# Graph attention on one core: scores computed with keys on the partitions, mask and sums on GpSimd

## The reference, cut to what matters

```
proj = x @ W                      # W: 256 x 512
Wh, Ws = split(proj, 2)           # 4096 x 256 each
scores = Wh @ Ws.T                # 4096 x 4096
a = softmax(scores, axis=-1) * adj
out = leaky_relu(a @ Wh + x, 0.01)
```

## Time and profile before

| | us |
|---|---|
| median of 3 runs | 2951.92 |
| lowest and highest run | 2949.37 to 2952.56 |
| span of the profiled execution, first to last instruction | 2948.1 |
| TensorE busy | 2849.7 (97%) |
| VectorE busy | 2153.3 (73%) |
| ScalarE busy | 1362.9 (46%) |
| GpSimd busy | 567.3 (19%) |

### The profile page before, as it was taken

How to read it: one execution, slowest core, us unless ns; L and a number is a source line. 1 busy time by engine, 2 the same in 40 slices (tenths; PEclk the granted TensorE clock), 3 DMA queues, 4 the chain that set the end, 5 groups by cost and what they waited for, 6 DMA issues and landing times. The chain is left out here.

```text
span 2948.1 us, 52591 instructions
## 1 busy us (share of the span) xinstructions
PE 2849.7 (97%) x16880; PEld 2497.7 (85%) x16880; DVE 2153.3 (73%) x3960; ACT 1362.9 (46%) x2417; POOL 567.3 (19%) x213
## 2 busy tenths in 40 slices
PE   4799999999999989999999999998999999999999
PEld 2699999999999978788888888887888888888888
DVE  7888888888888855666666666665566666676666
ACT  4566666666666646333333333334333333333333
POOL 5544545545544502000000000001100000000000
PEclk7899999999999999999999999999999999999999
DMA  2222222222222206333333333333533333333332
GB/s 97 82 75 78 80 70 74 82 71 78 75 72 78 75 30 225 102 103 104 107 100 98 97 104 100 107 102 101 161 100 104 102 109 103 112 111 102 103 104 72
DMA packets 120646, 283.62 MB, mean 96 GB/s; under 512 B 12816, under 2 KB 58640, under 8 KB 120592
## 3 DMA queue, kind: packets, MB, share of 16 engines
q1 hardware_dynamic: 113600, 264.29, 29.3%
q0 software_dynamic: 5120, 16.78, 1.7%
q10 hardware_dynamic: 1872, 1.84, 0.2%
HBM read 249.30 MB, written 33.55 MB: 96 GB/s over the span
## 5 line engine op out<-in xcount | busy, mean ns | idle before, releaser
L91 PE MATMUL l0b_acc<-l_h_parts,l0b_turned_hi 128*128 128x512 f32 x1984 | 759.2, 415 | 0.0
L480 POOL TENSOR_SCALAR l_adj_pieces<-l_adj_pieces 128x1024 f32<-128x1024 f32 x124 | 480.8, 3878 | 492.5 <-DMA l_adj_pieces<-in_adj_dram 492.3
L92 PE MATMUL l0b_acc<-l_h_parts,l0b_turned_lo 128*128 128x256 f32 x1984 | 556.5, 280 | 0.0
L498 ACT CAST l0b_turned_hi<-l0b_turn_psum 128x512 fp32r<-128x512 f32 x512 | 299.1, 585 | 340.6 <-PE l0b_turn_psum L663 335.6
L584 DVE TENSOR_TENSOR l0b_turned_lo<-l0b_turn_psum,l0b_turned_hi 128x512 fp32r<-128x512 f32 x512 | 351.7, 687 | 126.1 <-ACT l0b_turned_hi L498 122.4
L91 PEld LDWEIGHTS l0b_acc<-l_h_parts,l0b_turned_hi 128*128 128x128 f32 x1984 | 374.2, 189 | 66.2 <-issue 0.2
L1059 ACT CAST g1b_turned_hi<-g1b_turn_psum 128x512 fp32r<-128x512 f32 x256 | 149.9, 586 | 522.2 <-PE g1b_turn_psum L1173 521.7
L1059 ACT CAST g0b_turned_hi<-g0b_turn_psum 128x512 fp32r<-128x512 f32 x256 | 149.9, 585 | 521.2 <-PE g0b_turn_psum L1173 520.7
L92 PEld LDWEIGHTS l0b_acc<-l_h_parts,l0b_turned_lo 128*128 128x128 f32 x1984 | 375.1, 189 | 0.0
L91 PE MATMUL g1b_acc<-g_wh_parts,g1b_turned_hi 128*128 128x512 f32 x992 | 361.0, 398 | 0.6 <-DVE g1b_turned_lo L1098 0.5
L91 PE MATMUL g0b_acc<-g_wh_parts,g0b_turned_hi 128*128 128x512 f32 x992 | 361.0, 398 | 0.1
(11 more groups left out here) (191 smaller groups left out, 5708.1 us busy)
## 6 DMA issues: line engine op xcount, KB each, us to landing
g_adj_pieces<-in_adj_dram SPq DMA_DIRECT2D x256, 512.0 KB, 3.9
l_adj_pieces<-in_adj_dram SPq DMA_DIRECT2D x128, 512.0 KB, 3.9
g_wh_tile<-wh_tiles SPq DMA_DIRECT2D x64, 256.0 KB, 2.7
wh_tiles<-g0a_stage POOLq DMA_DIRECT2D x32, 256.0 KB, 3.3
wh_tiles<-g1a_stage POOLq DMA_DIRECT2D x32, 256.0 KB, 3.8
l0b_x_in<-in_x_dram SPq DMA_DIRECT2D x32, 128.0 KB, 3.2
x_rows<-l0b_x SPq DMA_DIRECT2D x32, 128.0 KB, 3.1
g0a_rows<-x_rows SPq DMA_DIRECT2D x8, 512.0 KB, 4.1
```

The costliest lines, as they stand in the source:

```text
L91: pe.matmul(out, lhs_hi, rhs, start=first, stop=False)
L92: return pe.matmul(out[:, width:], lhs_lo, rhs[:, :width], start=False, stop=False)
L480: pool.tensor_scalar(adj_pieces[:, q, :], adj_pieces[:, q, :], 0.0, PENALTY, ALU.is_le, ALU.mult).then_inc(penalty_ready, 1)
L498: act.copy(turned_hi[:, s % RING, :], turn_psum[:, s % RING, :]).then_inc(hi_ready, 1)
```

## The change

In stage b the scores are computed turned: keys on the partitions, queries along the free dimension. A block is 256 queries, a chunk is 4 tiles of 128 keys by 256 queries (128 partitions x 1024 elements); a layer has 16 blocks of 8 chunks, 128 chunks. The weights then need no transposes. Everything is unrolled. The maximum of a query, formerly a reduction along the free dimension, now takes elementwise maxima over the chunks, a fold, two transposes, a reduction, and a spread to all partitions by matmuls; the sum likewise. The adjacency is given a second time as an input in blocked and turned layout, prepared on the host. The work of chunk n is put in steps: its scores in step n, its shift, exponential and mask in step n+9, its split and its sum in step n+10, its product in step n+11. In stage a the stores of Wh move from GpSimd's queue to SyncE's, the fetch of the first adjacency goes ahead of the fetch of the first Wh, and the loops are unrolled.

```diff
+    BLOCK = 256
+    CHUNK = 4
+    PER = T // CHUNK
+    CHUNKS = BLOCKS * PER
+    SLOTS = 11
+    ADJ_SLOTS = 3
...
+                    for c in range(QUADS):
+                        load(c, c % 2)
+                        if c > 1:
+                            store_wh(c - 2, c % 2)
...
+                    for a in range(ADJ_SLOTS):
+                        fetch_adj(sp, a)
+                    sp.wait_ge(stage_out[0], 16 * PARTS)
+                    for b in range(2):
+                        fetch_wh(sp, b)
...
+            TO_SHIFT, TO_SPLIT, TO_WEIGH = 9, 10, 11
+            TURN_MAX, TURN_SUM = PER, PER - 1 + TO_WEIGH
+            STEPS = CHUNKS + TO_WEIGH
+            LATE = CHUNKS - PER
...
+                @block.gpsimd
+                def _(pool):
+                    def weight(c):
+                        piece = adj_ring[:, c % ADJ_SLOTS, :, :]
+                        pool.wait_ge(exp_made, c + 1)
+                        pool.wait_ge(adj_in[c % ADJ_SLOTS], 16 * (c // ADJ_SLOTS + 1))
+                        pool.tensor_tensor(piece, slab[:, c % SLOTS, :, :], piece, ALU.mult).then_inc(weighted, 1)
+
+                    def add_up(c):
+                        b, k = divmod(c, PER)
+                        pool.wait_ge(exp_made, c + 1)
+                        for e in range(2):
+                            if k == 0 and e == 0:
+                                wait(pool, sum_folded, b)
+                                pool.tensor_copy(sum_wide[:], half_of(c, e)).then_inc(summed, 1)
+                            else:
+                                pool.wait_ge(summed, 2 * c + e)
+                                pool.tensor_tensor(sum_wide[:], sum_wide[:], half_of(c, e), ALU.add
+                                                   ).then_inc(summed, 1)
...
+                    for n in range(STEPS):
+                        if 0 <= n - TO_SPLIT < CHUNKS:
+                            add_up(n - TO_SPLIT)
+                        if 0 <= n - TO_SHIFT < LATE:
+                            weight(n - TO_SHIFT)
...
+                @block.scalar
...
+                    for n in range(STEPS):
+                        if 1 <= n <= CHUNKS:
+                            take_half(n - 1, 1)
+                        if 0 <= n - TO_SPLIT < CHUNKS:
+                            high_part(n - TO_SPLIT)
+                        if 0 <= n - TO_SHIFT < CHUNKS:
+                            exponential(n - TO_SHIFT)
+                        if n < CHUNKS:
+                            take_half(n, 0)
...
+                @block.vector
...
+                        dve.tensor_tensor(max_wide[:], before, half_of(c, e), ALU.max).then_inc(max_step, 1)
...
+                        dve.tensor_tensor(chunk, chunk, neg_row[:].rearrange("p (o n) -> p o n", o=1).to_broadcast(
+                            [P, CHUNK, BLOCK]), ALU.add).then_inc(shifted, 1)
...
+                        dve.tensor_tensor(part_lo[:, c % 2, :, :], adj_ring[:, c % ADJ_SLOTS, :, :],
+                                          part_hi[:, c % 2, :, :].bitcast(F32), ALU.subtract).then_inc(lo_made, 1)
...
+                    for n in range(STEPS + 2):
+                        spreading, turning = block_at(n, TO_SHIFT), block_at(n, TURN_MAX)
+                        if spreading is not None:
+                            spread_row(spreading)
+                        if 0 <= n - TO_SHIFT < CHUNKS:
+                            shift(n - TO_SHIFT)
+                        if 1 <= n <= CHUNKS:
+                            join_max(n - 1, 1)
+                        if turning is not None:
+                            fold_max(turning)
+                        if 0 <= n - TO_SPLIT < CHUNKS:
+                            low_part(n - TO_SPLIT)
+                        if n < CHUNKS:
+                            join_max(n, 0)
+                        if turning is not None:
+                            negate_max(turning)
+                        if LATE <= n - TO_SHIFT < CHUNKS:
+                            weight(n - TO_SHIFT)
...
+                @block.tensor
...
+                    for n in range(STEPS):
+                        turning, adding = block_at(n, TURN_MAX), block_at(n, TURN_SUM)
+                        for q in range(CHUNK):
+                            if n < CHUNKS:
+                                score(n, q)
+                            if q == 1 and turning is not None:
+                                turn_max(turning)
+                            if q == 1 and adding is not None:
+                                turn_sum(adding)
+                            if q == 3 and turning is not None:
+                                spread(turning)
+                            if n >= TO_WEIGH:
+                                weigh(n - TO_WEIGH, q)
```

More of the change, by code:

```diff
@@ L840, in _ @@
+                    for b in range(2):
+                        fetch_wh(sp, b)
+                    if norm is not None:
                         for u in range(2):
                             sp.wait_ge(v_out[u], 8 * QUADS)
[L843 to L864, removed]
@@ L975, in attention_layer @@
[L975 to L983, removed]
-            acc = mem.psum("acc", [P, 2, 2 * D])
@@ L1061, in _, with take_half @@
-                    for q in range(PIECES):
-                        exponential(0, q, 0)
-                    def step(t, u, known):
-                        for g in range(GROUPS):
-                            split(t, g)
-                            if g < PIECES and known != T - 1:
-                                exponential(t + 1, g, 1 - u)
-                    pairs_of_tiles(act, T, 2, step)
+                    def take_half(c, e):
+                        act.wait_ge(score_made, 2 * c + e + 1)
+                        if e == 0:
+                            if c - SLOTS < LATE:
+                                wait(act, weighted, c - SLOTS + 1)
+                            wait(act, summed, 2 * (c - SLOTS + 1))
+                        act.copy(half_of(c, e), bank_of(c, e)).then_inc(score_taken, 1)
@@ L1168, in turn @@
-                    def turn(t, g, u):
-                        pe.wait_ge(weighted, PIECES * t + g * BANK // PIECE + 1)
-                        wait(pe, lo_ready, GROUPS * t + g - TURN_BANKS + 1)
-                        for k in range(TURNS):
-                            col = g * BANK + k * P
-                            last = pe.transpose(turn_psum[:, g % TURN_BANKS, k * P:(k + 1) * P],
-                                                rows[:, u, col:col + P], ident[:])
-                        last.then_inc(turns, 1)
@@ new lines, in turn_max, with spread @@
+                    def turn_max(b):
+                        pe.wait_ge(max_folded, b + 1)
+                        wait(pe, total_step, 2 * (b - 2) + 1)
+                        for i in range(SUBS):
+                            last = pe.transpose(turned_fold[:, i * P:(i + 1) * P], max_fold[:, i * P:(i + 1) * P],
+                                                ident[:])
+                        last.then_inc(max_turned, 1)
+                    def spread(b):
+                        pe.wait_ge(neg_lo_made, b + 1)
+                        wait(pe, neg_row_made, b)
+                        for i in range(SUBS):
+                            out = spread_max[:, i * P:(i + 1) * P]
+                            pe.matmul(out, neg_hi[:, i:i + 1].to_broadcast([P, P]), ident_r[:], start=True, stop=False)
+                            last = pe.matmul(out, neg_lo[:, i:i + 1].to_broadcast([P, P]), ident_r[:], start=False,
+                                             stop=True)
+                        last.then_inc(neg_spread, 1)
@@ L1209, in build @@
+def build(nc, x, adj, W, a, wtrans, w_stack, adj_blocks, out):
     N, D = x.shape
```

490 lines of the change are left out of this document (269 added, 221 removed).

## The result

The changed kernel takes **3431.49 us** (median of 4 runs, 3429.25 to 3432.82) against 2952.22 for the kernel before (median of 4, 2949.37 to 2952.56): ratio 1.1628, 95% interval 1.1611 to 1.1644. It is slower by 479 us; forecast were 395 (3347 us, range 3190 to 3500). (Where a run's time and its own span are both recorded, they differ by 1.8 to 2.1 us. So of the 3.8 us between the median and the profiled span before, which were put down to what lies around the instructions, some 2 belong to the profiled execution, which was faster than the median.)

What follows compares the result with a forecast made beforehand. TensorE bounds the kernel before; after the change, VectorE and GpSimd taking turns would. Stage b +195 and +190 in the two layers, starts +10, together +395 us, giving 3347 us, range 3190 to 3500.

Steps and rivals of the forecast that it cites:

- The turns: Stage b: VectorE's instructions with two SBUF inputs and GpSimd's tensor_tensors exclude each other, making a step 7.75 us.
- TensorE stays the bound: Rival for stage b: no exclusion, 5.68 us a step, 2858 us in all; faster below about 6.1 per step; chance 0.07.
- A turn lasts only while GpSimd reads: Rival for stage b: GpSimd's turn for two inputs 1.8 us instead of 2.35, chunk 7.1, total 3191; chance 0.08.
- The clock: Rival for stage b: TensorE's idle time lowers its clock, a step could grow to about 8.5 us, total 3527; chance 0.10.
- VectorE alone too full: Rival added with the experiments, no chance given: in stage b VectorE's own work, without exclusion by GpSimd, sets the time.
- 240 steps: Stage b, steps 9 to 128 of each layer, mask on GpSimd: 7.75 us each, 930 a layer.
- 30 blocks, beyond their steps: Stage b, 15 blocks a layer: fold, small instructions, slopes and wait for the spread, mostly given back: 1 us each.
- first score to first shift: Start of stage b: steps 0 to 8 with scores only, 26 us, and 1.5 for the first maximum's way through TensorE.
- late steps and end: Stage b, steps 129 to 136 with the mask on VectorE, 44 us, then last split, product, finishes and store, 12.
- stage a: Stage a: stores of Wh moved to SyncE's queue and unrolled loops, taken as 0.
- start of stage b: Between last projection and first score: adjacency loads ahead of Wh add 5 us a layer, between 0 and 12.
- the overlap per turn: Stage b: how far the paired VectorE and GpSimd instructions overlap, 0.26 us for each of three turns a step.

Runs made afterwards that it cites:

- Experiments 1: Changed kernel with the shift reading the spread maximum from PSUM instead of its SBUF copy, which is still made: 3200.8 us.
- experiment 2: Changed kernel with the shift reading the spread maximum and the running maxima reading the scores from PSUM instead of SBUF: 2964.2 us.
- experiment 3: Changed kernel with GpSimd's additions cut to 8 of 512 elements, leaving the sums out: 2981.7 us.
- 4: Changed kernel with the masks of all chunks on VectorE, the sums left on GpSimd: 3223.8 us.
- experiment 7: Changed kernel with shift and maxima reading PSUM, the maximum's cast and low part on ScalarE, first Wh fetched before adjacency and last store: 2896.72 us.
- Experiment 8: Changed kernel with the first block's maximum serving all 16 blocks, its path left out in 15, exponential scaled by 0.01: 3355.7 us.
- experiment 6: Changed kernel with the cast and low part of the negated maximum (128x2) on ScalarE instead of VectorE: 3433.7 us.
- experiment 5: Changed kernel with the stores of Wh back on GpSimd's queue and the first Wh fetched ahead of the adjacency: 3419.04 us.

## Why the prediction was right, and where it was short

**The mechanism holds.** The turns set the step, as the forecast had it. Experiments 1 and 2 take them away without less work, 3 and 4 shorten them from either side. TensorE's work, ScalarE's and the landing of the adjacency are hidden behind the turns.

**The rivals.** *TensorE stays the bound* fell at the step it named, 7.84 against its limit of 6.1. *A turn lasts only while GpSimd reads* fell: the second inputs of VectorE wait until GpSimd's tensor_tensor is nearly over, for 1024 and for 512 elements. *The clock* fell to 0.89 in stage b, but the step is accounted for by its turns, and VectorE never waits for TensorE in it; no run held the clock alone apart. *VectorE alone too full* fell by 3 and 4.

**The terms that were mis-sized.** The forecast was +395, the spans differ by 481.8.

| term | forecast, us | measured, us | off by |
|---|---|---|---|
| 240 steps | 7.75 each | 7.84 each | +22 |
| 30 blocks, beyond their steps | 1 each | 2.2 (g0b), 3.3 (g1b) | +53 |
| first score to first shift | 27.5 twice | 30.4 and 30.1 | +5 |
| late steps and end | 56 twice | 51.6 and 57.2 | -3 |
| stage a | 0 | 8.0 and 1.9 | +10 |
| start of stage b | 5 twice | 4.6 and 4.2 | -1 |

The sum is +86 of 87. The first shift comes 3 us later mostly because the first scores run at half clock: for 5 us from the first one on the granted clock is 0.50 (the record of 0.58 us above instead of 0.28), and the first 24 score matmuls take 5.3 us in g0b, where they take 2.9 in experiment 7, whose lead is 28.0.

```profile
1201.30:1206.30 5.00, 5.00 (x23) 5.00 (x24) 0.00 (x0) 0.59 (x1) 0.00 (x0) 0.50 0.18 67
```

*The step.* Two errors that nearly cancel, so that 7.75 came this near to 7.84 in part by luck: the shortest addition of 512 elements in this kernel took 1.34, not half of 2.35, which adds 0.33; and the overlap per turn is 0.34 rather than 0.26: in the two steps above, 2 x (2.35 + 2 x 1.34) + 2 x 3.82 = 17.7 less 15.67, over six turns. (In experiment 2 the shortest took 1.25; with that the two are 0.15 and 0.28.) The Trainium skill's figure (GPSIMD Engine Reference, Elementwise — side-by-side cycle accounting), from which the forecast estimated 1.27 for this addition, was nearer than half of 2.35. By the rule of the Trainium skill (SBUF — State Buffer, Who interferes with whom), exclusion without overlap, the step would be 8.85, or 8.67 with the addition at 1.25; the trace agrees with the exclusion and shows 0.28 to 0.34 us a turn less.

*The block.* This is the term that was furthest off, 1 us for 2.2 and 3.3. The forecast named the fold, the small instructions and VectorE's wait for the spread, and priced them away: "one maximum less and a copy in the place of an addition give most of it back". These give back about 1 us (0.69 for the maximum; the copy has a mean of 1.05 where an addition has 1.34 or more). And while the maximum goes through TensorE and back, both engines of the pair stand still for a part of the time. VectorE at the boundary of a block in g0b:

```profile
1744.06 2.44 DVE L1143 TENSOR_TENSOR g0b_max_fold<-g0b_max_wide 128x256 f32<-128x256 f32 x1
1746.43 2.29 DVE L1179 TENSOR_TENSOR g0b_part_lo<-g_adj_ring,g0b_part_hi 128x1024 fp32r<-128x1024 f32 x1
...
1751.56 0.42 DVE L1161 COPY g0b_neg_row<-g0b_side_psum 128x256 f32<-128x256 f32 x1 [1.48 <-PE g0b_side_psum L1269]
1752.09 1.23 DVE L1167 TENSOR_TENSOR g0b_slab<-g0b_slab,g0b_neg_row 128x1024 f32<-128x1024 f32 x1
```

VectorE waits 1.48 us for the spread, and GpSimd, which has no mask until the shift and its exponential are done, stands idle for 3.80 us before the mask at 1754.49. The next shift starts at 1757.79, 17.7 after 1740.05, where two steps take 15.7. Experiment 8 shows what the maximum's path costs as a whole (2.1 in g0b), and experiment 6 that the small instructions, which the forecast also named, are not it. What is left is the waiting and the fold, which takes 2.44 us for a width that takes 0.42 alone. VectorE's wait is 1.6 us a block on average (24.9 in 16, in the groups above), most of the 2.1; but that the waiting counts for more than the fold's turn is read from the timeline, and no run separates the two. In g1b some 0.6 more come from the finishing of a block: 63.4 against 62.8 in experiment 8, with the addition of x (mean 1.31 beside GpSimd, 0.42 in the kernel before).

*Stage a.* The stores were priced at 0 because SyncE's own order held up nothing. What was missed, in g0a, is the transfer itself: the load of x and its copy land later behind them (5.8 and 6.1 us instead of 4.1 and 2.8), and ScalarE waits for it 14.3 us in all in six quads of g0a, where it was 3.4 us once. The 1.9 us of g1a are the clock's (experiment 5).

## What to carry to other kernels

Before work is moved to GpSimd, list VectorE's instructions that read both operands from SBUF: each takes turns with GpSimd's tensor_tensors, and the price is the sum of both engines' records, not the larger. Where it must run beside GpSimd, give VectorE's instruction one operand in PSUM; here this was worth 467 of 3431 us with no work less. And price a chain once in a block by the engines that stand still while it runs as well as by its instructions.

## What the runs showed of the hardware beyond that

- The low part of the maximum, 128x2 elements on VectorE, took 0.16 us in the kernel after and 2.12 in g1b of experiment 2, where it falls beside GpSimd's work, and even the cast, with its one input in SBUF, took 1.71 in g0b of that run (0.76 in the kernel after). Taking them off VectorE was worth nothing in experiment 6 and 2.5 (g0b) and 1.3 us (g1b) a block on average between 2 and 7.
- GpSimd's tensor_tensors have little fixed share. The shortest took 0.19 us for 8 elements (experiment 3), 0.72 for 256, 1.25 for 512 and 2.34 for 1024 (experiment 2). The mean for 8 elements is 0.65 all the same: 75 of 240 in g0b took 0.2, nearly all others 0.6 to 1.2. So the waiting goes both ways, and GpSimd's short ones wait for VectorE's.
- The granted clock was 0.89 in stage b with TensorE busy in 79% and stood at 1.00 with 97% (g0b of experiment 7). A stage whose TensorE never waits, g1a, took 72.2 us or 74.2 with the same code, by how long the clock stayed at 0.50 at its start.
